# Sixteen-row attentions: the negated maxima turned in 32x32 blocks by VectorE and placed by four ScalarE copies

## The chip, the core and the metric

The kernel runs on one core of a Trainium2 chip. The metric is the device time of one execution in microseconds (us), here always the whole kernel. The core has five engines with a program each: TensorE (PE, matrix products, with its own loads of stationary operands, PEld), VectorE (DVE), ScalarE (ACT), GpSimd (POOL) and SyncE (SP), which issues DMAs. They meet only at semaphores: an engine that waits holds everything that stands behind in its own program.

## The reference, cut to what matters

x has 8 sequences of 512 tokens with 256 features, and eight layers are added to it in turn. The change touches the first three, L0x, L0f and L1x, which have the same core: 16 heads of 16 features, 512 queries against 512 keys.

```python
q = heads(layernorm(x) @ Wq.T + bq)            # keys and values from ctx (L0x, L1x) or from layernorm(x) (L0f)
attn = softmax(einsum('bhqd,bhkd->bhqk', q, k) / sqrt(16), axis=-1)
out = einsum('bhqk,bhkd->bhqd', attn, v)
x = x + out.reshape(B, -1, 256) @ Wo.T + bo    # L0f: q normalised and scaled first, out scaled by gates after
```

The softmax needs, for each head and query, the largest score of the 512.

## The kernel before, in words

One phase, `softmax_attentions`, runs 24 items (3 layers x 8 sequences; items of L0x and L1x are "cross", those of L0f "mixture"). Each item is 32 steps, numbered n; eight steps serve one group of four heads. Queries and keys are cut into bf16 parts that are stacked in 96 rows (`qstack`, `kstack`), so one bf16 product gives scores of near fp32 precision.

In each step PE computes two blocks of scores with queries on the partitions for the item's maxima (`for_maximum`, L760, into `ps_max`), 12 steps ahead (LEAD), and two blocks with keys on the partitions (`score`, L750, into `ps_sc`), whose exponentials ACT takes (L671). DVE reduces each block of `ps_max` to 128 maxima (L485). Both PSUM tiles have three banks, so product number i may not start before DVE (or ACT) has finished number i-3. After every fourth step PE multiplies the exponentials by the values (`values`, L774).

The maximum has to be subtracted before the exponential, and there it lies along the free axis of `ps_sc`. So when the 16 maxima blocks of a head group are there (step n%8==3) DVE writes their negatives as two bf16 parts (`negated`, L492 and L494). PE turns these with four small products against an identity into rows 96 to 103 of the single PSUM tile `ps_t` (L827), and ACT copies these rows, repeated for four heads, below the 96 rows of `qstack` (`take_negmax`, L684). The score product then reads 104 rows; in `kstack` the eight extra rows hold ones and zeros that select the right head's two parts (`own_key_rows`, L284). The first score of a group (n%8==0) waits for that copy.

The order of the work is written out by hand: `TURNS` lists at which step each use of `ps_t` (projections k, q, v, y, transposes xnT, hT, raw, qT, the gates and negmax) is made, on PE and on the engine that takes the result, and `shift` says for which item. A use of `ps_t` waits until the use before it has been taken. In each step PE does its fills first, then scores and maxima; DVE does what it takes from `ps_t` first, then its two maxima, then `negated`; ACT does its takes first, then its two exponentials. POOL makes the bf16 parts of queries and keys; its two series of an item may start when `negmax_ready` of a certain group has come.

Of the kernel before, what the change touches and what calls it, by code (L numbers as in the profile page):

```python
# [17 lines left out]
BF16 = mybir.dt.bfloat16  # L18
U32 = mybir.dt.uint32
ALU = mybir.AluOpType  # L20
# [3 lines left out]
P = 128  # L24
SEQS = 8
S = 512
D = 256
TILES = S // P
# [79 lines left out]
def rounds(steps):  # L108
# [5 lines left out]
    for number in range(-2, ITEMS + 1):  # L114
# [6 lines left out]
    "cross": [(4, "raw", 3), (5, "negmax", 1), (9, "v", 0), (10, "v", 1), (11, "hT", 0), (12, "hT", 1),  # L121
              (13, "negmax", 2), (14, "xnT", 0), (15, "raw", 0), (16, "y", 0), (17, "y", 1), (18, "xnT", 1),
              (19, "k", 0), (20, "k", 1), (21, "negmax", 3), (23, "raw", 1), (24, "q", 0), (26, "q", 1),
              (29, "negmax", 0), (31, "raw", 2)],
    "mixture": [(2, "v", 0), (3, "v", 1), (4, "raw", 3), (5, "negmax", 1), (7, "xnT", 0), (8, "xnT", 1),
                (9, "q", 0), (10, "q", 1), (11, "hT", 0), (12, "hT", 1), (13, "negmax", 2), (14, "k", 0),
                (15, "raw", 0), (16, "k", 1), (18, "gates", 0), (19, "qT", 0), (20, "qT", 1), (21, "negmax", 3),
                (22, "y", 0), (24, "y", 1), (25, "raw", 1), (29, "negmax", 0), (31, "raw", 2)],
# [9 lines left out]
def shift(what, c):  # L138

    if what in ("k", "xnT", "q", "qT"):  # L140
        return 2
    if what == "v" or (what, c) == ("negmax", 0):
        return 1
    if what in ("hT", "gates", "y") or (what, c) == ("raw", 3):
        return -1
    return 0


def softmax_attentions(nc, T, G, name, kind):
# [11 lines left out]
    LEAD = 12  # L161
    BANKS = 3
    SLOTS = 6
    PER = 4
    x_sb, ident, identb, own_rows = G["x"], G["ident"], G["identb"], G["own"]
    with Phase(nc, name) as ph:
# [25 lines left out]
        negmax = ph.sb("negmax", [P, 2, TILES, 4, 2], BF16)  # L192
# [45 lines left out]
        rden_ready = ph.sem("rden_ready")  # L238
        sp_step, sq_ready, qlen_ready = ph.sem("sp_step"), ph.sem("sq_ready"), ph.sem("qlen_ready")
# [197 lines left out]
        def _(dve):  # L437
# [50 lines left out]
            def negated(q, g):  # L488

                own = maxes[:, :, 4 * g:4 * g + 4]  # L490
                dve.wait_ge(max_taken, q.count(64, 16 * g + 16))
                V.tensor_scalar(negmax[:, g % 2, :, :, 0], own, -1.0, None, ALU.mult).then_inc(neg_step, 1)  # L492
# [2556 lines left out]
```

## Time and profile before

| quantity | us |
|---|---|
| median of 3 runs (4502.14 to 4506.45) | 4502.63 |
| profiled execution, its own time | 4504.13 |
| profiled execution, span of the trace | 4502.1 |
| PE busy in the span | 4233.5 (94%) |
| DVE busy | 2976.9 (66%) |
| ACT busy | 2544.5 (57%) |
| POOL busy | 810.4 (18%) |

The span runs from the first to the last instruction; 2.0 us of the profiled execution's own time lie around it. Busy PE means that a product is somewhere in the array: consecutive products overlap, so the start of one to the start of the next (0.22 us for a bf16 product of 512 columns) says more than its duration (0.38 us). The attentions of the change take the stretch from about 12 to 1762 us. A sum of waits over a stretch says little here, because three engines hand work to each other in a ring of three banks; one has to read places in the timeline.

### The profile page before, as it was taken

What the parts mean: (1) busy time and instruction counts of PE and PEld (TensorE: products, weight loads), DVE (VectorE), ACT (ScalarE), POOL (GpSimd) and SP (SyncE); (2) the same over time, 40 slices, a digit from 0 to 9 for tenths busy, and PEclk for the clock granted to TensorE, in tenths of its full rate; (3) what the DMA queues carried; (4) which work ended last, traced back from release to release, by engine and by line L of the source; (5) the groups of instructions that cost most, each with busy time, mean ns of one, the idle gap of its engine ahead of it and who ended that gap; (6) DMA issues with size and microseconds to landing.
All of it is one profiled execution on the core that took longest, in us unless ns stands there. A gap on an engine that the chain in (4) does not pass through costs nothing. (4 is left out here: it accounts for less than half of the span.)

```text
span 4502.1 us, 66443 instructions
## 1 busy us (share of the span) xinstructions
PE 4233.5 (94%) x23716; PEld 2403.0 (53%) x23750; DVE 2976.9 (66%) x7431; ACT 2544.5 (57%) x6408; POOL 810.4 (18%) x550
## 2 busy tenths in 40 slices
PE   6999999999999996778989999999999998999999
PEld 2344344444343343567545666666666665555555
DVE  5767777777767776867675666676776766344333
ACT  3767666666667765633555776767676775111111
POOL 2322444443322311523010000000000000000000
PEclk8999999999999998999999999999999999999999
DMA  8456455444456451000100110010101102000000
GB/s 161 73 76 87 65 63 85 54 69 63 74 75 84 69 71 61 1 15 15 75 12 27 31 32 28 30 36 26 33 27 32 32 27 73 5 5 5 10 5 10
DMA packets 182844, 204.97 MB, mean 46 GB/s; under 512 B 44651, under 2 KB 165099, under 8 KB 180854
## 3 DMA queue, kind: packets, MB, share of 16 engines
q1 hardware_dynamic: 180886, 199.15, 24.1%
q8 instruction: 192, 3.15, 0.3%
q10 hardware_dynamic: 1632, 1.57, 0.3%
q14 instruction: 134, 1.10, 0.1%
HBM read 139.90 MB, written 60.78 MB: 45 GB/s over the span
## 5 line engine op out<-in xcount | busy, mean ns | idle before, releaser
L485 DVE TENSOR_REDUCE L0x_maxes<-L0x_ps_max 128x1 f32<-128x512 f32 x1536 | 976.5, 683 | 291.0 <-PE L0x_ps_max L760 289.3
L671 ACT ACTIVATE L0x_probs<-L0x_ps_sc 128x512 f32<-128x512 f32 x1536 | 822.7, 607 | 362.3 <-PE L0x_ps_sc L750 358.3
L760 PE MATMUL L0x_ps_max<-L0x_kstack,L0x_qstack 96*128 96x512 bf16 x1536 | 588.0, 384 | 22.7 <-DVE L0x_maxes L485 21.3
L2756 ACT ACTIVATE L3x_pexp<-L3x_ps,L3x_nmax 128x77 f32<-128x77 f32 (+2 forms) x1536 | 601.4, 433 | 0.0
L750 PE MATMUL L0x_ps_sc<-L0x_qstack,L0x_kstack 104*128 104x512 bf16 x1536 | 557.7, 384 | 11.5 <-ACT L0x_probs L671 11.0
L2638 DVE TENSOR_REDUCE L3x_nmax<-L3x_ps 128x2 f32<-128x154 f32 (+2 forms) x768 | 346.3, 506 | 242.1 <-PE L3x_ps L2869 239.7
L2764 ACT COPY L3x_pT<-L3x_ps 128x512 f32<-128x512 f32 x512 | 275.1, 593 | 225.8 <-PE L3x_ps L2877 225.4
L2256 ACT ACTIVATE L3f_act_g<-L3f_ps_gu 128x512 f32<-128x512 f32 x128 | 76.4, 597 | 542.2 <-PE L3f_ps_gu L2302 542.1
L774 PE MATMUL L0x_ps_out<-L0x_probs,L0x_vpad 128*32 128x512 f32 x3072 | 371.0, 601 | 1.1 <-ACT L0x_probs L671 1.1
L2654 DVE TENSOR_SCALAR L3x_pexp<-L3x_pexp,L3x_rsum 128x77 f32<-128x77 f32 (+2 forms) x1536 | 357.7, 306 | 6.8
L2756 ACT ACTIVATION_READ_ACCUMULATOR L3x_pexp<-L3x_ps,L3x_nmax 128x1 f32 x1536 | 359.4, 235 | 0.0
L2199 DVE TENSOR_TENSOR L3f_h<-L3f_act_g,L3f_ps_gu 128x512 f32<-128x512 f32 x128 | 88.0, 687 | 383.1 <-ACT L3f_act_g L2256 382.9
L760 PEld LDWEIGHTS L0x_ps_max<-L0x_kstack,L0x_qstack 96*128 96x128 bf16 x1536 | 151.0, 98 | 282.5 <-DVE L0x_maxes L485 167.5
L2895 PE MATMUL L3x_ps<-L3x_pT,L3x_v 128*64 128x128 f32 x4096 | 279.9, 279 | 0.7 <-ACT L3x_oT L2772 0.7
L2877 PEld LDWEIGHTS L3x_ps<-ident,L3x_pexp 128*128 128x128 f32 x2048 | 239.1, 141 | 73.4 <-issue 55.5
L2877 PE MATMUL L3x_ps<-ident,L3x_pexp 128*128 128x128 f32 x2048 | 266.1, 273 | 0.9 <-DVE L3x_pexp L2654 0.9
L750 PEld LDWEIGHTS L0x_ps_sc<-L0x_qstack,L0x_kstack 104*128 104x128 bf16 x1536 | 150.6, 98 | 211.7 <-ACT L0x_probs L671 81.1
L2599 POOL TENSOR_TENSOR L3x_v<-L3x_v,L3x_relv 128x256 f32<-128x256 f32 x32 | 23.4, 731 | 1294.7 <-ACT L3x_v L2739 1294.7
L2302 PE MATMUL L3f_ps_gu<-L3f_xnT,L3f_wg 128*128 128x512 f32 x512 | 243.0, 597 | 2.1 <-DMA L3f_wd<-in_L3f_wd 2.1
L2313 PE MATMUL L3f_ps_y<-L3f_wd,L3f_h 128*128 128x256 f32 x1024 | 242.4, 380 | 1.5 <-DVE x_res L2209 1.5
L2895 PEld LDWEIGHTS L3x_ps<-L3x_pT,L3x_v 128*64 128x64 f32 x4096 | 218.3, 136 | 43.4 <-issue 42.5
L2302 PE MATMUL L3f_ps_gu<-L3f_xnT,L3f_wu 128*128 128x512 f32 x512 | 240.6, 592 | 0.0
(377 smaller groups left out, 6841.4 us busy)
## 6 DMA issues: line engine op xcount, KB each, us to landing
L0x_kstack<-parts_scratch SPq DMA_DIRECT2D x141, 256.0 KB, 10.0
L0x_qstack<-parts_scratch SPq DMA_DIRECT2D x141, 256.0 KB, 14.5
parts_scratch<-L0x_kparts SPq DMA_DIRECT2D x24, 768.0 KB, 3.7
parts_scratch<-L0x_qparts SPq DMA_DIRECT2D x24, 768.0 KB, 5.0
rel_scratch<-L3x_rel_e SPq DMA_DIRECT2D x32, 408.0 KB, 2.4
L3x_rel_d<-prob_scratch SPq DMA_DIRECT2D x32, 408.0 KB, 3.1
L0x_kv_in<-in_ctxT SPq DMA_DIRECT2D x16, 512.0 KB, 4.5
L3x_rel_t<-rel_scratch SPq DMA_DIRECT2D x32, 154.0 KB, 2.4
```

Source lines behind the costliest of these rows:

```text
L485: V.tensor_reduce(maxes[:, t, head:head + 1], ps_max[:, q.count(64, unit) % BANKS, :], AX.X, ALU.max).then_inc(max_taken, 1)
L671: nc.scalar.activation(probs[:, step % SLOTS, j], ps_sc[:, at % BANKS, :], ACT.Exp, scale=HD ** -0.5).then_inc(probs_ready, 1)
L750: nc.tensor.matmul(ps_sc[:, at % BANKS, :], kstack[q.parity][:, head, kt * P:(kt + 1) * P], qstack[q.parity][:, head, :], start=True, stop ...
L760: nc.tensor.matmul(ps_max[:, at % BANKS, :], qstack[q.parity][0:ROWS, head, t * P:(t + 1) * P], kstack[q.parity][0:ROWS, head, :], start=T ...
L774: i = nc.tensor.matmul(ps_out[32 * j:32 * j + 32, :], vpad[q.parity][:, kt, (HD + 1) * head:(HD + 1) * head + 32], probs[:, q.count(STEPS, ...
L2302: i = nc.tensor.matmul(ps_gu[:, n % 2, k], w[:, ci, n * P:(n + 1) * P], xnT[:, ci, :], start=(ci == 0), stop=(ci == C - 1))
L2638: i = V.tensor_reduce(nmax[:, n % 4, s], ps[:, bank:bank + 2, a:b], AX.X, ALU.max, negate=True)
L2654: i = V.tensor_scalar(pexp[:, m % 4, e, a:b], pexp[:, m % 4, e, a:b], rsum[:, m % 4, s, e:e + 1], None, ALU.mult)
L2756: i = nc.scalar.activation(pexp[:, n % 4, e, a:b], ps[:, SB + 2 * (n % 2) + e, a:b], ACT.Exp, bias=nmax[:, n % 4, s, e:e + 1], accum_out=s ...
L2764: nc.scalar.copy(pT[:, m % 2, e], ps[:, TB + e]).then_inc(pt_ready, 1)
L2877: i = nc.tensor.transpose(ps[:, TB + e, kt * P:(kt + 1) * P], pexp[:, m % 4, e, kt * P:(kt + 1) * P], ident[:])
L2895: i = nc.tensor.matmul(ps[DIMH * e:DIMH * (e + 1), OB, at:at + P], v[g % 2][:, vt, h * DIMH:(h + 1) * DIMH], pT[:, m % 2, e, kt * P:(kt + ...
```

## The change

The turn leaves PE and `ps_t`: the four products of L827 vanish from each of the 96 head groups and nothing else in PE's program moves. DVE zeroes a wider `negmax` once (32 columns per tile of queries instead of 8), writes the two parts into its first eight columns, and then turns the whole [128, 128] bf16 tile in 32x32 blocks (`V.transpose` into `neg_turned`). That leaves the eight rows of query block a (32 queries of each tile) on partitions 32a to 32a+7. ACT places them with one copy for each a, from SBUF, 8 partitions x 512 elements: a=0 and 1 at step n%8==5, a=2 at 6, a=3 at 7, each ahead of everything else that ACT has in that step. The four negmax entries of each item go out of `TURNS`. The first score of a group now waits for all four copies. The selecting rows of `kstack` (`own_key_rows`), which DVE and ACT wrote once in the run-up at step 16 of item -1, are written right at the start of the phase, ahead of their waits for the weights.

```diff
-    "cross": [(4, "raw", 3), (5, "negmax", 1), (9, "v", 0), (10, "v", 1), (11, "hT", 0), (12, "hT", 1),
-              (13, "negmax", 2), (14, "xnT", 0), (15, "raw", 0), (16, "y", 0), (17, "y", 1), (18, "xnT", 1),
...
+    "cross": [(4, "raw", 3), (9, "v", 0), (10, "v", 1), (11, "hT", 0), (12, "hT", 1),
+              (14, "xnT", 0), (15, "raw", 0), (16, "y", 0), (17, "y", 1), (18, "xnT", 1),
...
+    BLOCKS_AT = {5: (0, 1), 6: (2,), 7: (3,)}
...
-        negmax = ph.sb("negmax", [P, 2, TILES, 4, 2], BF16)
+        negmax = ph.sb("negmax", [P, 2, TILES, 32], BF16)
+        neg_turned = ph.sb("neg_turned", [P, 2, TILES, 32], BF16)
...
+            V.memset(negmax[:], 0.0).then_inc(negmax_blank, 1)
             statistics(Item(0), range(TILES))
             moments(Item(0))
+            dve.wait_ge(negmax_blank, 1)
             normalised(Item(0), range(TILES))
+            own_key_rows(V.tensor_copy, kstack[0]).then_inc(even_own_ready, 1)
             weights_here(dve, Item(0))
...
                 dve.wait_ge(neg_step, q.count(4, g + 1))
-                V.scalar_tensor_tensor(out=negmax[:, g % 2, :, :, 1], in0=own, scalar=-1.0,
-                                       in1=negmax[:, g % 2, :, :, 0], op0=ALU.mult,
-                                       op1=ALU.subtract).then_inc(negmax_ready, 1)
+                V.scalar_tensor_tensor(out=parts[:, :, :, 1], in0=own, scalar=-1.0, in1=parts[:, :, :, 0],
+                                       op0=ALU.mult, op1=ALU.subtract).then_inc(negmax_ready, 1)
+                dve.wait_ge(negmax_ready, group + 1)
+                if group >= 2:
+                    dve.wait_ge(negmax_placed, 4 * (group - 1))
+                V.transpose(neg_turned[:, g % 2].rearrange("p t r -> p (t r)"),
+                            negmax[:, g % 2].rearrange("p t c -> p (t c)")).then_inc(neg_blocks, 1)
...
+            own_key_rows(nc.scalar.copy, kstack[1]).then_inc(odd_own_ready, 1)
             weights_here(act, Item(0))
...
-            def take_negmax(q, g):
-
-                act.wait_ge(in_bank["negmax"], q.count(4, g + 1))
-                nc.scalar.copy(qstack[q.parity][ROWS:ROWS + 8, 4 * g:4 * g + 4, :],
-                               ps_t[ROWS:ROWS + 8, :].unsqueeze(1).broadcast_to([8, 4, S])
-                               ).then_inc(taken["negmax"], 1)
+            def place_negmax(q, g, blocks):
+
+                act.wait_ge(neg_blocks, q.count(4, g + 1))
+                rows = qstack[q.parity][ROWS:ROWS + 8, 4 * g:4 * g + 4, :].rearrange("k h (t a r) -> k h t a r", t=TILES, a=4)
+                for a in blocks:
+                    nc.scalar.copy(rows[:, :, :, a, :], neg_turned[32 * a:32 * a + 8, g % 2].unsqueeze(1)
+                                   .broadcast_to([8, 4, TILES, 32])).then_inc(negmax_placed, 1)
...
                 for n in range(STEPS):
+                    if n % 8 in BLOCKS_AT:
+                        owner, g = (q, n // 8 + 1) if n < 24 else (q.plus(1), 0)
+                        if owner.there:
+                            place_negmax(owner, g, BLOCKS_AT[n % 8])
                     for mine, w, c in due(q, n):
-                        if w == "negmax":
-                            take_negmax(mine, c)
...
-                    pe.wait_ge(taken["negmax"], q.count(4, g + 1))
+                    pe.wait_ge(negmax_placed, 4 * q.count(4, g + 1))
...
-                elif w == "negmax":
-                    pe.wait_ge(negmax_ready, q.count(4, c + 1))
-                    for t in range(TILES):
-                        i = nc.tensor.matmul(ps_t[ROWS:ROWS + 8, t * P:(t + 1) * P],
-                                             negmax[:, c % 2, t].rearrange("p h e -> p (h e)"), identb[:],
-                                             start=True, stop=True, tile_position=(0, ROWS))
```

DVE's program from step 11 of a cross item, before (L485 is the reduction, `xn` the normalisation, `maxes` its result):

```order
L463 TENSOR_SCALAR L0x_xn<-x_res,L0x_mv,L0x_rstd 128x256 x2
L485 TENSOR_REDUCE L0x_maxes<-L0x_ps_max 128x1 x2
L492 TENSOR_SCALAR L0x_negmax<-L0x_maxes 128x16
L494 SCALAR_TENSOR_TENSOR L0x_negmax<-L0x_maxes,L0x_negmax 128x16
L463 TENSOR_SCALAR L0x_xn<-x_res,L0x_mv,L0x_rstd 128x256 x2
L485 TENSOR_REDUCE L0x_maxes<-L0x_ps_max 128x1 x6
```

The same place on DVE after the change:

```order
L466 TENSOR_SCALAR L0x_xn<-x_res,L0x_mv,L0x_rstd 128x256 x2
L491 TENSOR_REDUCE L0x_maxes<-L0x_ps_max 128x1 x2
L502 TENSOR_SCALAR L0x_negmax<-L0x_maxes 128x4x4
L504 SCALAR_TENSOR_TENSOR L0x_negmax<-L0x_maxes,L0x_negmax 128x4x4
L509 STREAM_TRANSPOSE L0x_neg_turned<-L0x_negmax 128x128
L466 TENSOR_SCALAR L0x_xn<-x_res,L0x_mv,L0x_rstd 128x256 x2
L491 TENSOR_REDUCE L0x_maxes<-L0x_ps_max 128x1 x6
```

One instruction is added, between the negatives and everything that DVE owes to PE next.

ACT's program around steps 5 to 8 where a mixture item is being prepared, before (L684 is the one copy of the turned rows, L701 takes xnT and hT out of `ps_t`):

```order
L671 ACTIVATE L0x_probs<-L0x_ps_sc 128x512 x4
L684 CAST L0x_qstack<-L0x_ps_t 8x2048
L671 ACTIVATE L0x_probs<-L0x_ps_sc 128x512 x4
L701 COPY L0x_xnT<-L0x_ps_t 128x512
L671 ACTIVATE L0x_probs<-L0x_ps_sc 128x512 x2
L701 COPY L0x_xnT<-L0x_ps_t 128x512
```

The same place on ACT after the change:

```order
L683 ACTIVATE L0x_probs<-L0x_ps_sc 128x512 x4
L698 COPY L0x_qstack<-L0x_neg_turned 8x16x32 x2
L683 ACTIVATE L0x_probs<-L0x_ps_sc 128x512 x2
L698 COPY L0x_qstack<-L0x_neg_turned 8x16x32
L683 ACTIVATE L0x_probs<-L0x_ps_sc 128x512 x2
L698 COPY L0x_qstack<-L0x_neg_turned 8x16x32
L714 COPY L0x_xnT<-L0x_ps_t 128x512
L683 ACTIVATE L0x_probs<-L0x_ps_sc 128x512 x2
L714 COPY L0x_xnT<-L0x_ps_t 128x512
```

The one copy became two, one and one, spread over three steps, and the last stands ahead of the take of xnT.

## Rows read from the trace of the kernel before

**Rows 1.** Busy time by stretch: stretch, length, PE, PEld, DVE, ACT, POOL, PE clock, DMA, GB/s

```profile
200.00:1700.00 1500.00, 1427.93 (x7704) 609.37 (x7703) 1106.58 (x2244) 1006.41 (x1709) 517.35 (x256) 0.99 0.51 72
```

**Rows 2.** Groups by line and form, 100 to 1600 us: busy us, mean ns, idle before

```profile
L485 DVE TENSOR_REDUCE L0x_maxes<-L0x_ps_max 128x1 f32<-128x512 f32 x1353 | 860.9, 683 | 252.1 <-PE L0x_ps_max L760 250.6
...
L684 ACT CAST L0x_qstack<-L0x_ps_t 8x2048 bf16<-8x2048 f32 x85 | 157.9, 1858 | 11.2 <-PE L0x_ps_t L827 8.4
...
L827 PE MATMUL L0x_ps_t<-identb,L0x_negmax 128*8 128x128 bf16 x336 | 32.4, 218 | 15.7 <-DVE L0x_htok L513 8.3 <-DVE L0x_negmax L494 4.9 <-ACT L0x_qf L698 1.3
```

**Rows 3.** Timeline of PE, step 13 of a cross item: start us, length us, instruction

```profile
1245.48 0.38 PE L827 MATMUL L0x_ps_t<-identb,L0x_negmax 128*8 128x128 bf16 x4 [0.17 <-DVE L0x_negmax L494]
...
1246.63 0.39 PE L760 MATMUL L0x_ps_max<-L0x_kstack,L0x_qstack 96*128 96x512 bf16 x1
1246.95 1.92 PE L774 MATMUL L0x_ps_out<-L0x_probs,L0x_vpad 128*32 128x512 f32 x16
```

**Rows 4.** Timeline of DVE, the same moment

```profile
1244.94 0.18 DVE L492 TENSOR_SCALAR L0x_negmax<-L0x_maxes 128x16 bf16<-128x16 f32 x1
1245.16 0.18 DVE L494 SCALAR_TENSOR_TENSOR L0x_negmax<-L0x_maxes,L0x_negmax 128x16 bf16<-128x16 f32 x1
1245.25 0.73 DVE L463 TENSOR_SCALAR L0x_xn<-x_res,L0x_mv,L0x_rstd 128x256 f32<-128x256 f32 x2
1245.90 2.47 DVE L485 TENSOR_REDUCE L0x_maxes<-L0x_ps_max 128x1 f32<-128x512 f32 x4
```

**Rows 5.** Timeline of DVE at the start, the constant bf16 identity

```profile
2.83 0.23 DVE L919 CAST identb<-ident 128x128 bf16<-128x128 f32 x1 [1.90 <-DMA own<-in_own]
```

**Rows 6.** Timeline of PE and DVE, step 29

```profile
1215.50 0.38 PE L760 MATMUL L0x_ps_max<-L0x_kstack,L0x_qstack 96*128 96x512 bf16 x1
...
1214.28 2.48 DVE L485 TENSOR_REDUCE L0x_maxes<-L0x_ps_max 128x1 f32<-128x512 f32 x4
```

**Rows 7.** Timeline of PE and DVE, step 5 of a cross item

```profile
1229.13 0.38 PE L760 MATMUL L0x_ps_max<-L0x_kstack,L0x_qstack 96*128 96x512 bf16 x1
...
1228.01 1.88 DVE L485 TENSOR_REDUCE L0x_maxes<-L0x_ps_max 128x1 f32<-128x512 f32 x3
```

**Rows 8.** Timeline of PE and DVE, step 21 of a cross item

```profile
254.12 0.38 PE L760 MATMUL L0x_ps_max<-L0x_kstack,L0x_qstack 96*128 96x512 bf16 x1
254.43 0.39 PE L827 MATMUL L0x_ps_t<-identb,L0x_negmax 128*8 128x128 bf16 x4
254.75 0.39 PE L750 MATMUL L0x_ps_sc<-L0x_qstack,L0x_kstack 104*128 104x512 bf16 x1
...
254.10 1.99 DVE L485 TENSOR_REDUCE L0x_maxes<-L0x_ps_max 128x1 f32<-128x512 f32 x3 [1.05 <-PE L0x_ps_max L760]
```

**Rows 9.** One line of DVE: duration ns min/median/max, first and last start

```profile
L574 DVE SCALAR_TENSOR_TENSOR L0x_gpart<-L0x_gshare,L0x_gsw x8: 161/1744/1746, 750.0 to 1269.3; 128x4 f32<-128x4 f32 x8
```

**Rows 10.** `own_key_rows` on ACT: duration ns min/median/max, first and last start

```profile
L284 ACT CAST L0x_kstack<-own x16: 608/609/615, 43.1 to 50.9; 8x512 bf16<-8x512 f32 x16
```

**Rows 11.** Timeline of ACT and PE, steps 7 and 8, mixture item ahead

```profile
865.11 0.59 ACT L701 COPY L0x_xnT<-L0x_ps_t 128x512 f32<-128x512 f32 x1
...
865.75 0.66 PE L782 MATMUL L0x_ps_t<-ident,L0x_xn 128*128 128x128 f32 x4
```

**Rows 12.** Start: timeline of PE, then landing of the stacked queries (39 to 42 us)

```profile
52.14 3.78 PE L787 MATMUL L0x_ps_t<-L0x_kv_in,L0x_wk_cross 128*128 128x512 f32 x4 [7.90 <-ACT L0x_xnT L701]
...
58.52 0.81 PE L760 MATMUL L0x_ps_max<-L0x_kstack,L0x_qstack 96*128 96x512 bf16 x3
...
DMA to landing us min/median/max: 11.3/14.2/17.0
```

**Rows 13.** Waits, 100 to 1700 us, then one line of DVE as in rows 9

```profile
POOL L0x_qparts L373 <- DVE L0x_negmax L494: 116.3, 14, 9.2
POOL L0x_kparts L373 <- DVE L0x_negmax L494: 40.9, 8, 6.7
...
L492 DVE TENSOR_SCALAR L0x_negmax<-L0x_maxes x96: 178/179/1257, 70.1 to 1730.8; 128x16 bf16<-128x16 f32 x96
```

More of the change, by code:

```diff
@@ L120 @@
 TURNS = {
-    "cross": [(4, "raw", 3), (5, "negmax", 1), (9, "v", 0), (10, "v", 1), (11, "hT", 0), (12, "hT", 1),
-              (13, "negmax", 2), (14, "xnT", 0), (15, "raw", 0), (16, "y", 0), (17, "y", 1), (18, "xnT", 1),
[L123 to L128, printed above, removed]
+    "cross": [(4, "raw", 3), (9, "v", 0), (10, "v", 1), (11, "hT", 0), (12, "hT", 1),
+              (14, "xnT", 0), (15, "raw", 0), (16, "y", 0), (17, "y", 1), (18, "xnT", 1),
+              (19, "k", 0), (20, "k", 1), (23, "raw", 1), (24, "q", 0), (26, "q", 1),
+              (31, "raw", 2)],
+    "mixture": [(2, "v", 0), (3, "v", 1), (4, "raw", 3), (7, "xnT", 0), (8, "xnT", 1),
[3 rows of a table added]
 }
@@ L141, in shift @@
         return 2
-    if what == "v" or (what, c) == ("negmax", 0):
+    if what == "v":
         return 1
@@ L164, in softmax_attentions @@
     PER = 4
-    x_sb, ident, identb, own_rows = G["x"], G["ident"], G["identb"], G["own"]
+    x_sb, ident, own_rows = G["x"], G["ident"], G["own"]
     with Phase(nc, name) as ph:
@@ L490, in negated @@
                 own = maxes[:, :, 4 * g:4 * g + 4]
+                parts = negmax[:, g % 2, :, 0:8].rearrange("p t (h e) -> p t h e", e=2)
+                group = q.count(4, g)
                 dve.wait_ge(max_taken, q.count(64, 16 * g + 16))
[L492 removed]
+                if group >= 2:
+                    dve.wait_ge(neg_blocks, group - 1)
+                V.tensor_scalar(parts[:, :, :, 0], own, -1.0, None, ALU.mult).then_inc(neg_step, 1)
                 dve.wait_ge(neg_step, q.count(4, g + 1))
[L494 to L496 removed]
+                V.scalar_tensor_tensor(out=parts[:, :, :, 1], in0=own, scalar=-1.0, in1=parts[:, :, :, 0],
+                                       op0=ALU.mult, op1=ALU.subtract).then_inc(negmax_ready, 1)
+                dve.wait_ge(negmax_ready, group + 1)
+                if group >= 2:
+                    dve.wait_ge(negmax_placed, 4 * (group - 1))
+                V.transpose(neg_turned[:, g % 2].rearrange("p t r -> p (t r)"),
+                            negmax[:, g % 2].rearrange("p t c -> p (t c)")).then_inc(neg_blocks, 1)
             def take_v(q, half):
@@ L628, in steps @@
                         gate_scale(prev)
-                    if q.number == -1 and n == 16:
-                        own_key_rows(V.tensor_copy, kstack[0]).then_inc(even_own_ready, 1)
                     if not ahead.there:
@@ L725, in steps @@
                         take_out(q if n > 2 else prev, (n // 8 - 1) % 4)
-                    if q.number == -1 and n == 16:
-                        own_key_rows(nc.scalar.copy, kstack[1]).then_inc(odd_own_ready, 1)
                     if prev.there and not prev.cross and n == 19:
```

1 line of the change is left out of this document (added), and 3 rows, old and new, of the table TURNS.

## The prediction, made before the changed kernel ran

> **What bounds the kernel now.** Read the busy times of the attentions first: PE 95% of the stretch, DVE 74%, ACT 67% [rows 1]. That invites the sentence "PE is the bound, take work off it". The groups by line then show how little is at stake: the turn on PE is 4 products of 219 ns that overlap, and ACT's copy takes 1.86 us [rows 2]. Shares cannot say whether the time comes free, so I read the timeline at the four places of an item where the turn stands (steps 5, 13, 21, 29), and asked at each what the last product before the values (L774) waits for. The ring has three banks: the last product for the maxima of such a step (L760) can start only when DVE has ended the first reduction of that step. In step 13 that reduction starts at 1245.90 [rows 4] and takes 0.68 us [rows 2], so it ends at 1246.58, and the product starts at 1246.63 [rows 3]: DVE sets the time there, with 0.05 us of handing over. PE is busy and still not the bound. The places of the 24 items repeat closely, so one reading serves for many.
>
> **The change part by part.**
>
> *PE.* Per group the turn occupies PE from its start to the next score: 254.43 to 254.75, 0.32 us, and the wait in front of it goes too: the product before started at 254.12 and would have let go at 254.34 (0.22 us from start to start), so 0.41 us in all [rows 8]. Over 96 groups the bare products are 31 us.
>
> *DVE.* It gains one operation on the path of the reductions. No row shows a transpose. From below it is bounded by the smallest operation, 0.18 us (L494) [rows 4], and by 0.23 us for a cast of the same 128x128 shape [rows 5]; from above by the reduction of 512 elements, 0.68 us [rows 2]. A line through the two ends (16 and 512 elements) gives 1.02 ns an element and 0.29 us for 128; I take that, because the row nearest in shape, the cast, lies close to it. The path grows by more than the duration, since the transpose has to wait for L494 to end: L494 starts 0.22 us after L492 for the same reason, while L463 starts 0.09 us after L494, 0.09 us before it has ended [rows 4]. So 0.22 + 0.29 - 0.09 = 0.42 instead of 0.09, +0.33 us per group (from 0.22 at a duration of 0.18 to 0.72 at 0.68).
>
> The Trainium skill (VectorE: DVE Perf Modes, "The three transpose paths") gives a 128x128 bf16 transpose 0.31 us on VectorE against 0.39 us on TensorE; no row here shows the former, and by it the addition would be 0.35 us.
>
> Now the places, one for one. Step 13 of a cross item: DVE already bound, the values start 0.33 us later; 16 times, +5.3 us. Step 29: the first reduction starts at 1214.28; with 0.68, 0.05 and 0.33 the last product starts at 1215.34 instead of 1215.50 [rows 6], 0.16 us earlier; 24 times, -3.8 us. Step 5: 1228.01 + 0.68 + 0.05 + 0.33 = 1229.07 against 1229.13 [rows 7]; 24 times 0.06, -1.4 us. Step 21 of a cross item: DVE had waited 1.05 us for PE and does not decide [rows 8]; up to 0.41 us comes free, of which I take 0.30, since the exponentials of the scores are then 0.1 us late. This holds for 16 of 24; in the 8 items that follow a mixture item PE next waits for DVE's chain of gate operations, one of which alone takes 1.74 us in most [rows 9], and the gain is lost there. -4.8 us. Step 13 of the 8 mixture items has no normalisation on DVE beside it and I give it the same 0.30: -2.4 us.
>
> *ACT.* Four copies for one. The nearest row is the cast of 8x512 elements from SBUF to SBUF, 609 ns, sixteen of which start from 43.1 to 50.9, one each 0.52 us [rows 10]. So 4 x 0.52 = 2.1 us against 1.86 [rows 2]. Copies 0 and 1 stand where the old copy stood and copy 2 where ACT waits for PE, which is busy with the values for 1.9 us [rows 3]: both cost nothing. Copy 3 stands in the run of scores after the values and delays two exponentials by 0.5 us. In steps 7, 15 and 31 I cost that at nothing, because DVE's reductions are late there by as much; if that cover is missing it is 0.5 us a time (rival below). One place has no cover: where a mixture item is prepared, the take of xnT stands right behind copy 3, and PE's next use of `ps_t` waits for it (taken at 865.11 to 865.70, next fill at 865.75 [rows 11]). 8 times 0.5 us, +4.0 us.
>
> The Trainium skill prices this against the change (VectorE: DVE Perf Modes, "The TRN2 errata"): a fixed cost for each instruction that reads SBUF, 224 cycles on ScalarE against 172 from PSUM, so that many small tiles pay it each. Its formula gives 0.61 us for one copy, as rows 10 has it, and 2.45 us for four; the trace's spacing of 0.52 says that back to back they cost less. Where copies 2 and 3 stand alone, the longer figure is the right one; by it the 8 places would cost 0.1 us more each.
>
> *Start.* ACT's sixteen casts hold the take of xnT, and PE waits 7.90 us for it before the keys of item 1 (52.14) [rows 12]. Written at the start of the phase they lie beside the loads of the weights. But PE's first product for the maxima (58.52) also needs the stacked queries, and their last piece was issued at about 40.5 and took 17.0 us, to 57.5 [rows 12]. So 0.9 us at most comes free. Against it, PE then has its idle stretch directly ahead of those products and may enter them at the lower clock, which doubles the two projections of queries that follow (about 1.8 us each at the full clock). From -0.9 to +3.6; I take 0.
>
> *Sum.* 5.3 - 3.8 - 1.4 - 4.8 - 2.4 + 4.0 = -3.1 us. On the profiled execution's own 4504.13 (span 4502.1) that is 4501.0; this execution stood 1.5 us over the median of 4502.63, so 4499.5 for the median. A difference under 0.2%, 9 us, is what a measurement of this kernel does not tell from no change.
>
> **Rivals.**
>
> *PE is the bound after all.* For it: PE's 95% [rows 1], and each group takes a use of the single `ps_t` away, with the waits around it. Against it: the three places where L760 follows the reduction by 0.05 us or stands within 0.2 us of it. Time: at least the bare 0.32 us for 96 groups, 31 us, so 4472; with the waits (0.41) 39 us, 4463.
>
> *The last copy has no cover, slower.* Copy 3 holds the first score of the next group and two exponentials. It stands in 64 places beside the 8 already counted (three in each of 16 cross items, two in each of 8 mixture items). If DVE does not hide it, each costs up to 0.5 us, 32 us; half of them would be +16, and with the sum above 4515. All of them: 4531. It decides from about 0.2 us per place on, where the gains are used up and 9 us lost.
>
> *GpSimd holds the transpose, slower.* POOL's long operations of 1.9 to 2.1 us start just behind `negmax_ready`, 14 and 8 times [rows 13], and the transpose is issued at that moment. L492 normally takes 179 ns and once took 1257 [rows 13], and L574 takes 161 or 1744 [rows 9]: some operations of DVE wait while POOL works. If the transpose is of that kind, 22 places lose about 1.6 us, 35 us in all: 4534. Against it: the reductions keep their 683 ns mean over the whole stretch with POOL at work for a third of it [rows 1, 2]. The Trainium skill (GPSIMD Engine Reference, "Key points") names as sensitive the instructions in a 2-port mode or with two inputs in SBUF; the transpose has one input, and no run so far shows its mode.
>
> *The start is more than I think.* If the first item could begin as soon as PE is ready, 7.9 us would come free: 4492. The landing at 57.5 speaks against it.
>
> **How the numbers follow.** Forecast (near no change) 0.53, PE bound 0.21, copy 3 uncovered 0.15, GpSimd 0.08, the start 0.03. The forecast's own range is 4490 to 4509: its DVE term moves by 0.33 us at 64 places between the ends of the duration as follows, -0.11 x 64 = -7 us and +0.39 x 64 = +25 us, of which I keep a third. The range over all cases is 4470 to 4522: it takes in most of the PE rival and the smaller half of the copies and leaves about 0.2 outside. Faster by over 9 us: 0.21 + 0.02 + 0.11 of the forecast's own case = 0.34. Slower by over 9 us: 0.08 + 0.10 + 0.05 = 0.23. Within: 0.43.
>
> **What would show it.** The page after has no L827 and 96 transposes near 0.29 us; 0.7 or more than 1 us would break the DVE term. At step 13 of cross items the last product before the values still stands 0.05 us behind a reduction, and from the negatives to the values is 0.33 us longer; at step 21 it is 0.3 shorter. The four copies are 0.61 us each. ACT's 7.90 us in PE's waits at the start is gone while the first product for the maxima stands within 1 us of where it was. If all four places are shorter by 0.3 or more, the reading that DVE holds them was wrong.

## The result, and the profile after

The changed kernel takes 4512.51 us (median of 20 runs, 4507.06 to 4518.52), the kernel before 4503.90 us (20 runs, 4500.31 to 4506.72): ratio 1.0020, 95% interval 1.0014 to 1.0026. It is slower by 9 us where 3 us less were forecast. The profiled execution took 4515.56 us with a span of 4513.8 us.

PE's part did shrink. These are busy times by stretch, with the columns of [rows 1], and groups by line and form as in [rows 2], both of the kernel after:

```profile
200.00:1700.00 1500.00, 1398.94 (x7315) 586.90 (x7317) 1118.69 (x2315) 1052.33 (x1948) 517.04 (x256) 0.99 0.51 71
```

```profile
L491 DVE TENSOR_REDUCE L0x_maxes<-L0x_ps_max 128x1 f32<-128x512 f32 x1346 | 853.6, 681 | 231.0 <-PE L0x_ps_max L772 230.0
L772 PE MATMUL L0x_ps_max<-L0x_kstack,L0x_qstack 96*128 96x512 bf16 x1346 | 514.4, 382 | 43.6 <-DVE L0x_maxes L491 42.3
L762 PE MATMUL L0x_ps_sc<-L0x_qstack,L0x_kstack 104*128 104x512 bf16 x1345 | 488.5, 383 | 24.3 <-ACT L0x_qstack L698 11.9 <-ACT L0x_probs L683 10.4 <-issue 0.5
L698 ACT COPY L0x_qstack<-L0x_neg_turned 8x512 bf16<-8x512 bf16 x336 | 206.5, 615 | 8.7 <-DVE L0x_neg_turned L509 0.5
L509 DVE STREAM_TRANSPOSE L0x_neg_turned<-L0x_negmax 128x128 bf16<-128x128 bf16 x84 | 26.2, 311 | 2.9
```

PE is 29 us less busy in the stretch, ACT 46 us and DVE 12 us more. Three things follow. The transpose takes 311 ns in the mean (0.29 us was forecast), and none of the 96 more than 314, so the rival "GpSimd holds the transpose" is out. The reductions are as long as before [rows 2]. And PE has a new wait in front of the scores, 11.9 us for L698, the copies on ACT, where the kernel before shows 7.8 us in the same group and all of it for the exponentials:

```profile
L750 PE MATMUL L0x_ps_sc<-L0x_qstack,L0x_kstack 104*128 104x512 bf16 x1352 | 489.6, 382 | 7.8 <-ACT L0x_probs L671 7.8
```

Where the 9 us arise can be read place by place, because cross rounds repeat within about 0.02 us. I took the start of the first score of each step, relative to the first score of its item, in both traces, and subtracted (median over seven cross items, 3 to 5 and 18 to 21; items are numbered from 0, and a round is the time from one item's first score to the next one's). In rounds 10 to 13 the places repeat as well, but for steps 24 to 28, behind the chain of gate operations: there the single rounds lie from -0.83 to +1.35, and the median says little:

```
place in a round of cross items    forecast   measured (after minus before, us)
step 5                              -0.06      -0.05
steps 7 and 8                        0         +0.25
step 13                             +0.33      +0.32
step 21                             -0.30      -0.29
step 29                             -0.16      -0.14
step 31, first score of the next     0         +0.18
round                               -0.19      +0.27

a round with mixture items (10 to 14)
step 5                              -0.06      -0.04
steps 6 to 8, copy 3 ahead of xnT   +0.5       +0.76
step 13                             -0.30      -0.25
step 21                              0         -0.27
steps 24 to 28, behind the gates     0         +0.17
step 29                             -0.16      -0.14
step 31                              0         +0.11
```

A step may look late only because the first score of its own round was late; "steps 7 and 8" and "step 31, first score of the next" are what stays after that has evened out. In cross rounds four places came out as forecast, and two that were put at nothing did not. Step 13 first; timeline of the kernel after (start, length, instruction, and in brackets the idle time before it and who ended it), the place of [rows 3, 4]:

```profile
1251.43 0.18 DVE L502 TENSOR_SCALAR L0x_negmax<-L0x_maxes 128x16 bf16<-128x16 f32 x1
1251.64 0.18 DVE L504 SCALAR_TENSOR_TENSOR L0x_negmax<-L0x_maxes,L0x_negmax 128x16 bf16<-128x16 f32 x1
1251.86 0.31 DVE L509 STREAM_TRANSPOSE L0x_neg_turned<-L0x_negmax 128x128 bf16<-128x128 bf16 x1
1252.09 0.70 DVE L466 TENSOR_SCALAR L0x_xn<-x_res,L0x_mv,L0x_rstd 128x256 f32<-128x256 f32 x2
...
1253.45 0.39 PE L772 MATMUL L0x_ps_max<-L0x_kstack,L0x_qstack 96*128 96x512 bf16 x1 [0.81 <-DVE L0x_maxes L491]
...
1253.77 1.06 PE L786 MATMUL L0x_ps_out<-L0x_probs,L0x_vpad 128*32 128x512 f32 x8
```

From the first negative to the values 2.34 us pass, against 2.01 in [rows 3, 4]: +0.33, and the last product for the maxima still waits for DVE. Step 5 of item 19 is of the same kind after the change: the reduction starts at 1446.11, and the product at 1446.85, after a wait of 0.42 us for it.

Now steps 7 and 8 of item 19. Before, PE's last wait there is for DVE:

```profile
1442.02 0.38 PE L750 MATMUL L0x_ps_sc<-L0x_qstack,L0x_kstack 104*128 104x512 bf16 x1
1442.24 0.38 PE L760 MATMUL L0x_ps_max<-L0x_kstack,L0x_qstack 96*128 96x512 bf16 x1
...
1442.45 0.38 PE L750 MATMUL L0x_ps_sc<-L0x_qstack,L0x_kstack 104*128 104x512 bf16 x1
1443.16 0.39 PE L760 MATMUL L0x_ps_max<-L0x_kstack,L0x_qstack 96*128 96x512 bf16 x1 [0.33 <-DVE L0x_maxes L485]
```

The kernel after, the same place:

```profile
1450.84 0.61 ACT L698 COPY L0x_qstack<-L0x_neg_turned 8x512 bf16<-8x512 bf16 x1
...
1451.47 2.06 ACT L683 ACTIVATE L0x_probs<-L0x_ps_sc 128x512 f32<-128x512 f32 x4
...
1451.51 0.39 PE L762 MATMUL L0x_ps_sc<-L0x_qstack,L0x_kstack 104*128 104x512 bf16 x1 [0.52 <-ACT L0x_qstack L698]
...
1451.73 0.38 PE L772 MATMUL L0x_ps_max<-L0x_kstack,L0x_qstack 96*128 96x512 bf16 x1
1452.13 0.39 PE L762 MATMUL L0x_ps_sc<-L0x_qstack,L0x_kstack 104*128 104x512 bf16 x1
1452.35 0.38 PE L772 MATMUL L0x_ps_max<-L0x_kstack,L0x_qstack 96*128 96x512 bf16 x1
```

The first score of step 8 needs all four copies of its group. Copy 3 ends at 1451.45 and the score starts at 1451.51; the maxima come in one order with the scores and shift too. DVE's 0.33 us of cover is gone (1452.35 shows no wait) and 0.25 us stay. The same stands at the turn to the next item, where 0.18 us stay:

```profile
1505.64 0.61 ACT L698 COPY L0x_qstack<-L0x_neg_turned 8x512 bf16<-8x512 bf16 x1
...
1506.31 0.39 PE L762 MATMUL L0x_ps_sc<-L0x_qstack,L0x_kstack 104*128 104x512 bf16 x1 [0.24 <-ACT L0x_qstack L698]
```

Where a mixture item is prepared [rows 11], copy 3 holds the take of xnT and the take holds PE:

```profile
869.26 0.61 ACT L698 COPY L0x_qstack<-L0x_neg_turned 8x512 bf16<-8x512 bf16 x1
869.90 0.59 ACT L714 COPY L0x_xnT<-L0x_ps_t 128x512 f32<-128x512 f32 x1
...
870.53 0.66 PE L794 MATMUL L0x_ps_t<-ident,L0x_xn 128*128 128x128 f32 x4 [0.59 <-ACT L0x_xnT L714]
```

### The profile page after: what moved, and what is told of

It reads as the page before. It is cut to its first block and busy times, and to the rows that moved or that the text cites. A ratio compares the mean times of both kernels' runs of the same rounds, so it can differ in the third digit from the quotient of the medians.

```text
span 4513.8 us, 66153 instructions
## 1 busy us (share of the span) xinstructions
PE 4213.3 (93%) x23332; PEld 2382.0 (53%) x23366; DVE 2999.9 (66%) x7528; ACT 2603.8 (58%) x6696; POOL 808.8 (18%) x550
## 5 line engine op out<-in xcount | busy, mean ns | idle before, releaser
L762 PE MATMUL L0x_ps_sc<-L0x_qstack,L0x_kstack 104*128 104x512 bf16 x1536 | 558.8, 384 | 31.5 <-ACT L0x_qstack L698 14.8
L698 ACT COPY L0x_qstack<-L0x_neg_turned 8x512 bf16<-8x512 bf16 x384 | 236.0, 615 | 12.7 <-DVE L0x_neg_turned L509 3.3
```

Source lines behind the costliest of these rows:

```text
L762: nc.tensor.matmul(ps_sc[:, at % BANKS, :], kstack[q.parity][:, head, kt * P:(kt + 1) * P], qstack[q.parity][:, head, :], start=True, stop ...
```

## The experiments

All times below are medians of runs beside the kernel before, which took 4502.0 to 4503.7 us in these comparisons; the kernel after stands at ratio 1.0020.

**Copy 3 one step earlier.** `BLOCKS_AT` of the changed kernel:

```diff
-    BLOCKS_AT = {5: (0, 1), 6: (2,), 7: (3,)}
+    BLOCKS_AT = {5: (0, 1), 6: (2, 3)}
```

> Copy 3 is moved from step 7 to step 6 of each group of eight, right behind copy 2; nothing else differs from the changed kernel. Theory (the last copy holds the first score): in cross items the first score of step 8 stands 0.25 us later against the step before than it did, and the first score of the next item 0.17 us, because it waits for copy 3; in items that prepare a mixture item steps 6 to 8 are 0.76 us longer because copy 3 stands ahead of a take of xnT. Behind copy 2 ACT waits 0.47 us for a score, so copy 3 delays one exponential by 0.14 us and all three losses go: 16 x 0.42 = 6.7 us, and 8 x 0.76 = 6.1 us unless the gate chain takes them: 4500 to 4506 against 4512.5 of the changed kernel, that is no slower than before. Rival (the turn on DVE is the cost): nothing of DVE changes, 4511 to 4513.

Measured 4504.92 us, ratio 1.0005 (0.9996 to 1.0014): about 7 us under the kernel after, with nothing of DVE changed, so the rival falls. The steps: 0.01 us instead of 0.25 at steps 7 and 8, 0.05 instead of 0.18 at the next item, 0.00 instead of +0.76 at steps 6 to 8 of rounds that prepare a mixture item. But a cross round gained only 0.09 us, since 0.28 us appeared at step 24. The timeline shows why:

```profile
1474.99 0.59 ACT L683 ACTIVATE L0x_probs<-L0x_ps_sc 128x512 f32<-128x512 f32 x1
...
1475.61 1.25 ACT L698 COPY L0x_qstack<-L0x_neg_turned 8x512 bf16<-8x512 bf16 x2
...
1476.89 2.06 ACT L683 ACTIVATE L0x_probs<-L0x_ps_sc 128x512 f32<-128x512 f32 x4
...
1477.54 0.39 PE L762 MATMUL L0x_ps_sc<-L0x_qstack,L0x_kstack 104*128 104x512 bf16 x1 [0.47 <-ACT L0x_probs L683]
```

At step 22 ACT has no idle time: two copies behind one another delay the exponentials that the last score of step 23 needs.

**Copy 3 where each group can bear it.**

```diff
+    BLOCKS_AT = {5: (0, 1), 6: (2, 3), 21: (0, 1), 22: (2,), 23: (3,)}
...
-                    if n % 8 in BLOCKS_AT:
+                    blocks = BLOCKS_AT.get(n if n // 8 == 2 else n % 8)
+                    if blocks:
```

> Copy 3 stands in steps 6, 14 and 30 but in step 23 for the last group (with copy 3 in step 6 of every group, the first score of step 24 came 0.28 us later per cross item, since two copies at step 22 hold the exponentials that the scores of step 23 wait for; in step 23 it costs nothing there). Theory: per cross item +0.18 - 0.28 = -0.10 us against before, 16 x 0.28 = 4.5 us under the kernel with copy 3 in step 6 everywhere: 4500 (ratio to before 0.9995). Rival: the 0.28 us only moves to another wait, 4505.

Measured 4503.94 us, ratio 1.0001 (0.9992 to 1.0010). Each steady cross round is 0.09 us shorter than before, as expected (-0.10), and PE's wait for the copies from 100 to 1600 us falls from 11.9 to 1.6. The whole did not fall by 4.5 us. In the profiled executions the first item takes 2.2 us more than with copy 3 in step 6, and the last item 1.8 us more (3.8 above the kernel before, against 2.0), on which more below.

**Without copy 3.**

```diff
-    BLOCKS_AT = {5: (0, 1), 6: (2,), 7: (3,)}
+    BLOCKS_AT = {5: (0, 1), 6: (2,)}
...
-                    pe.wait_ge(negmax_placed, 4 * q.count(4, g + 1))
+                    pe.wait_ge(negmax_placed, 3 * q.count(4, g + 1))
```

> The changed kernel without copy 3 after item 1 (a quarter of each item's selecting rows keeps what an earlier item left there). Theory: cross items give 0.25 us at step 7 and 0.17 us at step 31, items that prepare a mixture item 0.76 us at steps 6 to 8, of which the gate chain takes a part: 16 x 0.42 + 8 x (0.4 to 0.76) = 10 to 13 us, 4500 to 4502. Rival: copy 3 is covered and costs only the 8 x 0.5 us of the prediction: 4508.

In the first two items copy 3 is still made, inside step 6, by an edit not shown here. Measured 4499.80 us, ratio 0.9994 (0.9985 to 1.0002). The steps give 0.00 us at steps 7 and 8, 0.00 at the next item and 0.00 at steps 6 to 8 of rounds that prepare a mixture item. In the last item, 1.1 us longer after the change, it is 0.1 us shorter than before. The surpluses at steps 6 to 8 and at the next item are copy 3 and nothing else; it costs about 12 us in all (0.0026 of the time).

**DVE's part alone**, added to the kernel before:

```diff
+                group = q.count(4, g)
+                dve.wait_ge(negmax_ready, group + 1)
+                if group >= 1:
+                    dve.wait_ge(idle_done, group)
+                V.transpose(idle_out[:], idle_in[:]).then_inc(idle_done, 1)
```

> The kernel before, with one 128x128 bf16 transpose of a scratch tile added on DVE behind each pair of negatives (it waits for the second negative, and nobody waits for it). PE's turn and ACT's single copy stay. This is DVE's part of the change alone. Theory: at step 13 of the 16 cross items the values start 0.31 to 0.33 us later, at steps 5, 21 and 29 PE's own turn is later than DVE and hides it: +5 us, 4509. Rival, DVE sets the time at every place: 96 x 0.33 = 32 us, 4536. Rival, GpSimd holds the transpose: 22 x 1.6 = 35 us, 4539. If DVE's part costs nothing: 4504.

Measured 4517.20 us, ratio 1.0033 (1.0021 to 1.0046): 14.8 us instead of 5. Each steady cross round is 0.67 us longer, 0.33 at step 13 and 0.33 at step 5; rounds with mixture items 0.33, at step 5. My reading that PE's own turn was later than DVE at step 5 had missed what the turn waits for:

```profile
1448.38 0.31 DVE L506 STREAM_TRANSPOSE L0x_idle_out<-L0x_idle_in 128x128 bf16<-128x128 bf16 x1
1448.61 0.22 DVE L521 RECIPROCAL L0x_rden<-L0x_ps_t 128x16 f32<-128x16 f32 x1
1448.87 0.43 DVE L523 TENSOR_TENSOR L0x_htok<-L0x_ps_t,L0x_rden 128x256 f32<-128x256 f32 x1
...
1449.35 0.39 PE L837 MATMUL L0x_ps_t<-identb,L0x_negmax 128*8 128x128 bf16 x4 [0.48 <-DVE L0x_htok L523]
```

The turn on PE needs the single `ps_t`, which DVE frees behind the negatives. In this kernel all that is put on DVE there passes into PE. In the changed kernel the two parts nearly cancel: in the next experiment, which has neither, step 5 is 0.37 us shorter than before, and the transpose takes 0.32 back, which is why step 5 came out at -0.05 as forecast.

**The changed kernel without the transpose.**

```diff
-                V.transpose(neg_turned[:, g % 2].rearrange("p t r -> p (t r)"),
-                            negmax[:, g % 2].rearrange("p t c -> p (t c)")).then_inc(neg_blocks, 1)
```

> The changed kernel without DVE's transpose: ACT copies from the negatives themselves (the values placed are not the turned ones; nothing else is left out). Theory A (DVE's 0.33 us is on the path where the ring of maxima waits for it): in the kernel after, the last product for the maxima stands 0.06 us behind a reduction at steps 5, 13 and 29 too, so these come 0.33, 0.33 and about 0.25 us earlier; 16 x 0.91 + 8 x 0.58 = 19 us, 4493. Rival B (DVE's addition counts at step 13 of cross items alone, as the prediction had it): 16 x 0.33 = 5 us, 4507.

Measured 4497.53 us, ratio 0.9991 (0.9982 to 1.0000), 13 us under the kernel after. Theory A holds in place: steps 5, 13 and 29 come 0.32, 0.32 and 0.27 us earlier. Its 19 us were too many, since 0.27 us of each cross round goes back at the first score of the next item, which then waits 0.52 us for copy 3. Rival B is put there as the prediction's view; in fact the prediction let DVE decide at steps 5 and 29 too.

**The start.** Own key rows back at step 16 of the first round, in the changed kernel:

```diff
-            own_key_rows(nc.scalar.copy, kstack[1]).then_inc(odd_own_ready, 1)
             weights_here(act, Item(0))
...
+                    if q.number == -1 and n == 16:
+                        own_key_rows(nc.scalar.copy, kstack[1]).then_inc(odd_own_ready, 1)
```

(and the same for DVE's). Three kernels get this edit: the changed one, the one with copy 3 in step 6 and the one with copy 3 where each group can bear it. The kernel before gets the opposite one, the early casts alone:

> The sixteen casts of own key rows of each parity go back to step 16 of the first round; the turn stays as in the changed kernel. Theory: the start costs 1.6 us (first score of item 1 stands 1.58 us later than before), so 4511. Rival, the casts' place frees the 7.9 us that PE waited: 4520. Rival, the lost 3.4 us of item 0 are all the clock's and stay away here: 4509.

> Both edits together: copy 3 in step 6 and the own key rows back at step 16. Theory: the two gains add, 4498 to 4504, and this one is the fastest of the four. If the start is worth nothing, the same as with copy 3 moved alone.

> Copies as in the kernel with copy 3 in steps 6, 14, 30 and 23, and the own key rows back at step 16 of the first round. Theory of the start: in the six kernels that write the own key rows at the start, the core is at the lower clock again at about 60 us, under the two projections of queries, and 16.8 to 17.9 us pass from the first product for the maxima to the first score, against 15.4 to 15.7 us in the four that write them in step 16; the keys of item 1 come 2 to 4 us earlier there. So the interval is 15.7 here, and the total the same within 2 us: 4502 to 4505. If the start move costs time on balance, 4501.

> The kernel before with the own key rows alone written at the start of the phase; the turn stays on PE. Theory: the last piece of the stacked queries decides, not ACT: within 2 us of before, 4501 to 4505, and the spread is that of the stretches at the lower clock. Rival, PE's 7.9 us wait comes free: 4495. Rival, the move costs what item 0 lost in the kernel after: 4506.

Measured 4518.70 us, ratio 1.0032 (1.0020 to 1.0045); 4505.51, ratio 1.0005 (0.9996 to 1.0014); 4504.89, ratio 1.0003 (0.9994 to 1.0012); 4506.40, ratio 1.0006 (0.9998 to 1.0015). Against the kernel that differs in the start alone, the late casts are +0.0012 (the intervals overlap), 0 and +0.0002, the early ones in the kernel before +0.0006: all four lie within their intervals of nothing, from 5 us gained to 3 us lost by the early casts. Neither 7.9 us nor 3.4 us is told apart from that. The traces show two effects of opposite sign. The wait for ACT is gone, and one for a transfer stands in its place, in the kernel after (compare [rows 12]):

```profile
51.01 3.64 PE L799 MATMUL L0x_ps_t<-L0x_kv_in,L0x_wk_cross 128*128 128x512 f32 x4 [5.19 <-DMA L0x_kv_in<-in_ctxT]
...
59.46 0.82 PE L772 MATMUL L0x_ps_max<-L0x_kstack,L0x_qstack 96*128 96x512 bf16 x3 [2.05 <-DMA L0x_qstack<-parts_scratch]
...
63.42 3.62 PE L799 MATMUL L0x_ps_t<-L0x_xnT,L0x_wq_cross 128*128 128x512 f32 x4
```

From the first product for the maxima to the first score 16.8 to 18.0 us pass in the ten profiles with the early casts, 15.4 to 15.9 us in the seven without. The projection at 63.42 is 3.62 us long, where in the kernel before it is 1.88: a stretch at the lower clock, 1.2 instead of 2.4 GHz, lies under it. Busy times by stretch, first of the kernel before, then of it with the move alone (clock: the third column from the end):

```profile
56.00:70.00 14.00, 10.88 (x30) 3.80 (x30) 9.81 (x16) 2.71 (x4) 8.04 (x4) 0.99 1.10 341
```

```profile
56.00:70.00 14.00, 11.08 (x22) 3.81 (x23) 6.69 (x12) 1.52 (x3) 8.03 (x4) 0.76 1.10 312
```

A second execution of the kernel before shows 0.89 in this stretch, between the two, and its interval is 15.4 us all the same. The prediction had named both effects (-0.9 to +3.6, taken as 0), and no pair of kernels contradicts its 0.

**Each of the two kernels once more**, as they are.

> A second look at the changed kernel. If the steady places are the mechanism, each cross item is again 0.25 to 0.27 us longer than before and the items 7 to 9 again 0.4 us; if the 2.17 us of item 16 and the 1.09 us of the last item are the clock's, they differ from the first look.

> A second look at the kernel before, for the spread of the start, of the items with the gate chain and of the last item; cross items should repeat within 0.03 us.

They took 4513.73 and 4503.66 us. Cross rounds repeat: +0.26 or +0.27 us each after, 0.00 to 0.02 between the two executions of before. The first score of item 1 does not: 3.0 us apart between the two executions of before, 4.6 us between those of after, which I put down to the loads. Two more places are longer after the change.

*Items 15 and 16.* In both executions of after the core falls to the lower clock once, behind step 18 of item 16 in the one and of item 15 in the other, and 1.6 us are lost; in both of before it doesn't. But the kernel with DVE's part alone, where PE keeps its turn, falls to it too (item 15, 1.7 us). So the missing turn is not needed for it, and the drop may not belong to this change alone.

*The last item.* It is 1.1 and 4.1 us longer after, 0.0 between the two of before. These are two losses. The first 1.1 us are the same in both executions, most of them at steps 24 and 25, and they are not the clock's, which stood at 2.4 GHz in the first. No item follows whose maxima would be computed beside, so from step 20 on the scores run against ACT alone, and a copy there is covered by nothing; without copy 3 the 1.1 us are gone. Kernel after, first execution:

```profile
1746.72 0.61 ACT L698 COPY L0x_qstack<-L0x_neg_turned 8x512 bf16<-8x512 bf16 x1
1747.35 2.06 ACT L683 ACTIVATE L0x_probs<-L0x_ps_sc 128x512 f32<-128x512 f32 x4
...
1747.39 0.39 PE L762 MATMUL L0x_ps_sc<-L0x_qstack,L0x_kstack 104*128 104x512 bf16 x1 [0.74 <-ACT L0x_qstack L698]
```

The other 3.0 us are at the lower clock and come in the second execution alone. The last 20 us of the item, before, after, and after in the second execution:

```profile
1728.70:1748.70 20.00, 16.23 (x97) 4.94 (x99) 3.78 (x10) 16.77 (x31) 0.00 (x0) 1.00 0.00 1
```

```profile
1740.10:1760.10 20.00, 15.06 (x89) 4.59 (x92) 3.21 (x9) 16.71 (x33) 0.00 (x0) 1.00 0.00 1
```

```profile
1738.70:1758.70 20.00, 16.12 (x81) 4.22 (x76) 1.36 (x4) 13.76 (x27) 0.00 (x0) 0.83 0.00 1
```

0.83 is a mean over stretches at 2.4 and at 1.2 GHz. Of the 13 profiles without PE's turn seven fall to the lower clock in the last item, for 1.5 to 3.2 us; of the four with it none does.

**DVE's three operations apart.** In the kernel with moved copies one reduction stands between each two of them:

```diff
                     if own.there:
                         maximum(own, 2 * (m % STEPS))
+                    if pending:
+                        second_part(*pending)
+                    if own.there:
                         maximum(own, 2 * (m % STEPS) + 1)
-                        if m % 8 == 7:
-                            negated(own, (m % STEPS) // 8)
+                    if pending:
+                        blocks_turned(*pending)
+                    if own.there and m % 8 == 7:
+                        first_part(own, (m % STEPS) // 8)
+                        turning.append((own, (m % STEPS) // 8))
```

> DVE's three operations of the turn (negative, second negative, transpose) are no longer back to back: one reduction for the maxima stands between each two, so that the wait of one for the end of the one before is covered; the copies start after the exponentials of step 5 (copies 0 to 3 in step 6, for the last group 0 to 2 in step 22 and 3 in step 23). Theory: of the 0.33 us and of the 0.22 us between the two negatives, 0.12 us each is waiting, so 0.24 us less on DVE's path at steps 5, 13 and 29, where the ring of maxima waits for DVE: 16 x 0.6 + 8 x 0.4 = 13 us under the kernel with the moved copies: 4491. Rival: the transpose then ends 1.9 us later and ACT's copies with it, and the first score behind them pays what DVE saves: 4500 to 4510.

> The same with the own key rows back at step 16 of the first round. Theory: within 2 us of the kernel with the interleaved operations alone, 4490 to 4493; the interval from the first product for the maxima to the first score is 15.7 us instead of 17 or more.

Measured 4537.17 us, ratio 1.0078 (1.0064 to 1.0091), and 4537.87, ratio 1.0077 (1.0064 to 1.0090): the rival, and more than it said. The steps show both halves. Steps 5 to 12 are 0.43 us and steps 29 to 31 0.28 us shorter than with the operations together, but steps 14 to 16 lose 3.2 us in four of the seven cross rounds and 1.7 us in the other three. Most of the 1.7 us is one instruction, though no kernel takes it out alone. Put off by one reduction, the second negative, an operation with two inputs in SBUF, meets a long operation of POOL and ends when that ends (307.06):

```profile
304.69 2.37 POOL L367 TENSOR_TENSOR x_res<-x_res,L0x_bo_cross 128x1024 f32<-128x1024 f32 x1 [7.52 <-DVE L0x_xn L466]
305.12 1.98 DVE L511 SCALAR_TENSOR_TENSOR L0x_negmax<-L0x_maxes,L0x_negmax 128x16 bf16<-128x16 f32 x1
```

It takes 0.17 us as a rule, and 1.39 to 1.98 us in 17 of its 96 places; before the change and with moved copies it never took more than 0.18. The transpose, the four copies and the take of xnT are late behind it, and PE waits 2.2 us for that take. In every second round PE then runs at the lower clock (0.58 from 312 to 314; the projection L826 takes 3.45 us, in the rounds between 1.99): these are the other 1.5 us. That group was left together next, on the reading that the transpose's place behind a normalisation was to blame (`if n == 11:` calls all three parts at once, its copies in 13 and 14):

> As the interleaved kernel, but for the group whose rows are placed at step 13 DVE's three operations stay back to back and the copies stay in steps 13 and 14. In the fully interleaved kernel steps 5 to 12 and 29 to 31 came out 0.42 and 0.27 us shorter per cross item than with back-to-back operations, while the step behind 13 lost 3.7 us, since the transpose there came out behind a normalisation and the copies behind the takes. Theory (DVE's waits count at 5 and 29, the late copies only behind 13): 16 x 0.69 = 11 us and up to 8 x 0.4 in the others under the kernel with moved copies (4504): 4490 to 4493, faster than before by 0.2 to 0.3%. Rival: what is gained is lost at the next wait inside the item: 4500 to 4504.

Measured 4503.47 us, ratio 1.0000 (0.9991 to 1.0010). Cross rounds are 0.66 us shorter than before, as expected; rounds 6 to 15 lose it again, 5.2 us against the kernel before, up to 2.0 us at step 24. Here is the chain of gates on DVE before, with POOL's operations between them, and then in this kernel (timelines):

```profile
975.46 2.14 POOL L375 TENSOR_TENSOR L0x_kf<-L0x_kf,L0x_kparts 128x1024 f32<-128x1024 f32 x1
...
977.07 0.56 DVE L570 TENSOR_TENSOR L0x_gsw<-L0x_gexp,L0x_grec 128x8 f32<-128x8 f32 x1
...
977.68 1.90 POOL L378 TENSOR_TENSOR L0x_kparts<-L0x_kf,one 128x1024 bf16<-128x1024 f32 x1
...
977.85 1.75 DVE L574 SCALAR_TENSOR_TENSOR L0x_gpart<-L0x_gshare,L0x_gsw 128x4 f32<-128x4 f32 x1
```

```profile
970.33 2.13 POOL L378 TENSOR_TENSOR L0x_kf<-L0x_kf,L0x_kparts 128x1024 f32<-128x1024 f32 x1
...
971.21 1.27 DVE L595 TENSOR_TENSOR L0x_gsw<-L0x_gexp,L0x_grec 128x8 f32<-128x8 f32 x1
...
972.54 1.90 POOL L381 TENSOR_TENSOR L0x_kparts<-L0x_kf,one 128x1024 bf16<-128x1024 f32 x1
...
972.72 1.75 DVE L599 SCALAR_TENSOR_TENSOR L0x_gpart<-L0x_gshare,L0x_gsw 128x4 f32<-128x4 f32 x1
```

Each of these DVE operations ends when POOL's does: 977.07 + 0.56 = 977.63 and 975.46 + 2.14 = 977.60; 971.21 + 1.27 = 972.48 and 970.33 + 2.13 = 972.46. In the second kernel DVE arrives 0.7 us earlier relative to POOL (0.88 us behind its start instead of 1.61) and only waits longer. That explains a gain of nothing, not a loss. The loss is POOL's start: its series waits for the second negative (`negmax_ready`), which this kernel puts off by one reduction. In rounds 9 to 13 POOL starts 1.47 us behind the first negative, in the kernel before, in the changed one and in the one with moved copies 0.47; and in all of them DVE's take of y behind the gates (`ffo`) starts 8.53 to 8.55 us after POOL. So the chain ends 0.5 to 1.0 us later than with moved copies. How much of the rest at step 24 is the clock was not taken apart.

**Apart in rounds of cross items alone** (`if n == 11 or not only_cross(q):`, the copies placed by the same test):

> As the kernel interleaved but at step 13, and only in rounds where no item between the one before and the one two ahead is a mixture item (13 rounds of 24); the other rounds stand as in the kernel with moved copies. Theory: those rounds stay 0.57 us shorter each than with moved copies (-0.66 against -0.09 us), and the rounds with the gate chain no longer pay the 1 to 2 us at step 24 that the interleaved one lost there: 4504 - 13 x 0.57 = 4497, 0.15% faster than before. Rival: the start and the end of the attentions at the lower clock eat it: 4501 to 4504.

Measured 4494.25 us, ratio 0.9982 (0.9973 to 0.9991): faster than the kernel before, and the lowest median of all. The steady rounds stand at -0.66 us.

## Why the prediction was wrong

*Step that failed: copy 3 costed at nothing at steps 7, 15 and 31*, "because DVE's reductions are late there by as much". It was right for step 15 (0.00) and wrong for 7 and 31, 0.25 and 0.18 us in cross rounds (16 x 0.43 = 6.9 us) and 0.11 us at step 31 of mixture rounds (8 x 0.11 = 0.9 us). I looked for who held PE's products for the maxima (DVE) and called copy 3 hidden behind them. But the score that opens the next group waits for copy 3 itself, and PE issues scores and maxima in one order. The cover was real and too small: 0.33 us against a copy of 0.61 us. And in the last item, with no products for the maxima beside the last scores, there was none: some 0.9 us more than in another cross round. The rival "the last copy has no cover" named the mechanism, with a chance of 0.15. That its half case (4515) lies near the 4512.5 measured is in part luck: it had 16 us for the copies at these places, which cost about 9, and none of what follows here.

*Mis-sized: copy 3 ahead of the take of xnT.* 0.76 us for 0.5: it delays both takes, of steps 7 and 8. 8 x 0.26 = 2.1 us more.

*No term: the clock behind the start.* 1.6 us once at items 15 and 16, nothing or 3.0 us in the last item. With all of these -3.1 becomes 9.3 or 12.3; from the first score of item 1 to the last score the two executions measured 9.9 and 13.2, and the rest, under 1 us, has no term. (Both executions lie above the median of 4512.51.) What brings the lower clock stays open. At items 15 and 16 the work that PE no longer does is not the only cause, since the kernel with only DVE's part shows it too. For the last item it may be (seven of 13 profiles without that work, none of four with it), but no kernel gave PE only that work back.

*Right:* DVE bounds step 13 (+0.32 for 0.33); steps 29 and 5, where DVE sets the time after the change (-0.14 and -0.05 for -0.16 and -0.06); step 21 (-0.29 for -0.30); the transpose's duration; GpSimd does not hold it. The gate chain takes the gain of step 21 in mixture rounds in the main (+0.17 of the 0.27 in the median). *Wrong, but not in the prediction:* that DVE's part alone would be hidden behind PE's turn at step 5. PE's turn waits there for DVE, and that kernel pays 14.8 us, not 5.

## What to carry to other kernels

Before you call a new operation hidden, name every instruction that waits for its result and every one queued behind it, and compare its length with the cover at each: half a cover is half a cost. When work moves from a busy engine to two others, the gain is spent where those were last already; here only a placing found for each group of heads turned -3.1, then +9, into -8 us. An engine held by another until a fixed moment (DVE by POOL in the gate chain) gives back whatever is saved ahead of it, and if what you put off also starts the other engine, you lose. Before you move an instruction, look what runs on the other engines at its new place: 0.17 us became 1.98.

## What the runs showed of the hardware

- ACT's copies of 8x512 bf16 take 613 to 618 ns and start 0.64 us apart back to back (1.25 us for two), where the sixteen casts of [rows 10] had started every 0.52 us; the difference was not looked into.
- DVE's 128x128 bf16 transpose took 311 to 314 ns at each of 96 places of the changed kernel, and 298 to 314 in the fastest one, beside POOL's long operations too (at 1043.79 in the kernel with moved copies, POOL from 1043.83). Small DVE operations with two inputs in SBUF were held until POOL's ended: L570 and L574 in the gate chain, and in the interleaved kernel the second negative in 17 of 96 places, each time to within 0.04 us of POOL's end. The first negative, with one input, was held in 1 to 6 of 96 places (0.50 to 1.76 us for 0.18).
- Two profiles of one kernel differ by 0.02 us in a steady round of 68 us, so a difference of 0.1 us per round can be read where the whole time, spread over 6 to 13 us, cannot tell it.
